# DVE's attention loop begins 21 instructions later in its stream

## The chip, the cores and the metric

The kernel runs on one core of a Trainium2 chip. The metric is the device time of one execution in microseconds, and the median of the runs is taken. The core has a matrix engine (PE, TensorE), whose weight loads are shown apart as PEld, a vector engine (DVE), a scalar engine (ACT), GpSimd (POOL) and SyncE (SP), which only issues transfers and waits. Each engine runs an instruction stream of its own, and the streams meet only at semaphores. The instructions are themselves fetched by DMA, on queues of their own (q14 and q8 in the profile).

## What is computed

A batch of 32 elements with 112 tokens of 512 numbers passes through cross-attention with 16 heads against 375 context rows, and then through a mixture of 8 experts of which each token takes two.

```python
x = x + _L0_xattn_ref(_layernorm(x), ctx_2048, mask, wq, bq, wk, bk, wv, bv, wo, bo)
x = x + _L0_ffn_ref(_layernorm(x), gate_up_proj, down_proj, router_w)

# _L0_xattn_ref: q and the output projection are quantized to 8 bits, k and v are not
q = _w8a8_linear(x, wq, bq); k = cond @ wk.T + bk; v = cond @ wv.T + bv
scores = jnp.einsum('bhnd,bhld->bhnl', q, k) * inv_sqrt_d + mask[:, None]
attn = jax.nn.softmax(scores, axis=-1)
o = jnp.einsum('bhnl,bhld->bhnd', attn, v)
return _w8a8_linear(o, wo, bo)

# _L0_ffn_ref: for each expert, weighted by the router's share of the token
gate, up = jnp.split(h @ gup.T, 2, axis=-1)
y = jax.nn.silu(gate) * up @ dp.T
```

## The kernel before

The kernel has three stages in a row: the weights are prepared (to about 34 us in the profile), attention and routing run over the batch (to about 1284 us), and then the experts run over tiles of 128 tokens.

The change is in the attention stage. All five engines follow one software pipeline there, written out by hand. In step `it` an engine works on several batch elements at once: the projections of element `it + 1`, scores, softmax and values of element `it`, the output projection of `it - 1`, and layer norm and routing of `it - 2`. Within a step each engine goes through the 16 heads in order. For one head the path is:

- PE computes `score` (L726) from `q_stack` and `k_stack`.
- DVE adds the mask and takes the minimum, an instruction that writes `probs` and a read of its accumulator that writes `neg_max` (L575). It is the first arithmetic of a step on DVE.
- ACT takes the exponential, `probs` (L499), which needs `neg_max`.
- PE turns `probs` (L734), ACT copies `probs_t` out (L492), and PE multiplies with `v` (L746).

Two banks hold scores, and PE may not compute a score before DVE has read the one two heads back (`masked`). Between the heads PE computes the projections of the next element (L761, L766).

Each engine runs the steps through the helper `iterations` (L324). Steps -3 to 2 are written out, steps 3 to 28 run in a hardware loop (`eng.Fori`), two steps a pass and 13 passes, and steps 29 to 33 are written out again. Elements 3, 5, 7 and so on to 27 start a pass. The loop's registers are set and its branch stands at L329. The waits in the loop are against a register, computed by instructions at L314. There is no barrier at the end of a pass: each engine branches back by itself. The helper `waited` (L320 to L322) is one instruction that raises a semaphore, `waits_taken`, on which nobody waits; the kernel uses it to carry a wait ahead of an instruction that has no room for it.

The streams of the built program are, in instructions of one loop body: PE 582, DVE 309, ACT 182, SP 139, POOL 96.

Of the kernel before, what the change touches and what calls it, by code (L numbers as in the profile page):

```python
# [212 lines left out]
def attention(nc, W, R, x, ctx_t, mask, x1, h2, slots):  # L213
# [19 lines left out]
    with ExitStack() as ctx:  # L233
# [72 lines left out]
        waits_taken = sem("waits_taken")  # L306
        routed, ranked, weighing, grown_made, entered = sem("routed"), sem("ranked"), sem("weighing"), sem("grown_made"), sem("entered")
        ROUTE, WEIGH = 11, 6
        counted, tabled = sem("counted"), sem("tabled")

        def need(eng, s, count):
# [8 lines left out]
        def waited(eng):  # L320

            eng.sem_inc(waits_taken, 1)  # L322

        def iterations(eng, body):  # L324

            lo, hi = 3, B - 3 - (B - 6) % 2
            for it in range(-3, min(lo, B + 2)):
                body(it, it)
            with eng.Fori(0, (hi - lo) // 2) as j:  # L329
                for k in range(2):  # L330
                    body(j * 2 + (lo + k), lo + k, True)
            for it in range(hi, B + 2):
                body(it, it)
# [215 lines left out]
        def _(dve):  # L549
            def quantize(src, amax, scale, inv, shift, ints, chain, base):  # L550

                need(dve, chain, base)
                dve.tensor_scalar(scale, amax, 1.0 / QMAX, QEPS, ALU.mult, ALU.max).then_inc(chain, 1)
                need(dve, chain, base + 1)
                dve.reciprocal(inv, scale).then_inc(chain, 1)
                need(dve, chain, base + 2)
                dve.tensor_scalar(shift, src, inv, ROUND, ALU.mult, ALU.add).then_inc(chain, 1)
                need(dve, chain, base + 3)
                dve.tensor_scalar(ints, shift, ROUND, None, ALU.subtract).then_inc(chain, 1)

            def body(it, par, inside=False):
# [4 lines left out]
                for h in range(H):  # L566
# [116 lines left out]
                    if h == 14 and has_nn:  # L683
                        need(dve, q_made, 3 * (nn - 1) + 1)
                        quantize(x_in[:, p, :], x_amax[:, :], x_scale[:, p:p + 1], x_inv[:, :], shifted[:, :], x_int[:, :], ln1, 8 * nn + 4)

            iterations(dve, body)

            def table(n, ins):
# [400 lines left out]
def program(nc, x, ctx_t, mask, wq, bq, wk_t, bk, wv_t, bv, wo, bo, gate_up_t, down_t, router_t, out):  # L1090
# [10 lines left out]
    with ExitStack() as ctx:  # L1101
# [22 lines left out]
        with ExitStack() as first:  # L1124
            sb = lambda name, shape, dt=F32: first.enter_context(nc.sbuf_tensor(name, shape, dt))
            W.update({n: sb(n, [128, 4, C], BF16) for n in ("wq_int", "wo_int")})
            W.update({n: sb(n, [128, C]) for n in ("wq_row", "wo_row", "bq_row", "bv_row", "bo_row")})
            W.update(bk_col=sb("bk_col", [128, 4]), router=sb("router", [128, 4, E]), minus_half=sb("minus_half", [128, 1]))
            W.update(stage=sb("ctx_stage", [128, 4, LP]), x_in=sb("x_in", [N, 2, C]))
            W.update(width=width, prio=sb("prio", [128, E]), regions=sb("regions", [128, E]), token=sb("token", [N, 1]),  # L1130
                     taken=sb("taken", [128, E], BF16), ones=sb("ones", [128, E]), minus_one=sb("minus_one", [128, 1]),
                     tile_no=sb("tile_no", [128, width]), tile_row=sb("tile_row", [128, width]),
                     before=sb("before", [128, 128], BF16), ones16=sb("ones16", [128, 128], BF16),
                     taken_sum=sb("taken_sum", [N, E], BF16))
            W.update({n: first.enter_context(nc.semaphore(n)) for n in ("ctx_in", "x_in_ld", "stage_pad", "c_hi_made", "c_lo_made",
                                                                        "slots_cleared", "pads_cleared")})
            prepare_weights(nc, W, x, ctx_t, wq, wk_t, wv_t, wo, bq, bk, bv, bo, router_t, slots, h2, out[T:T + PAD_ROWS, :])
            attention(nc, W, R, x, ctx_t, mask, out[0:T, :].rearrange("(b n) c -> b n c", n=N),
                      h2[0:T, :].rearrange("(b n) c -> b n c", n=N), slots)
# [29 lines left out]
```

## Time and profile before

| | |
|---|---|
| median of 3 runs | 1750.88 us (1750.59 to 1752.73) |
| the profiled execution, its time | 1751.63 us |
| its span, first to last instruction | 1749.9 us |
| PE busy | 1534.1 us, 88% |
| DVE busy | 941.4 us, 54% |
| ACT busy | 881.9 us, 50% |
| POOL busy | 732.9 us, 42% |
| granted clock of PE, mean | 0.94 of full speed |

The page gives busy shares over the whole span. They don't say which engine a stage waits for: for that the waits of an engine in a stretch are read, each with what ended it. "Issue" there stands for an idle stretch that no semaphore ended. The instructions that the sequencer handles alone (branches, registers, semaphores) are not busy time, but have their start times in the trace, and they are what shows where in its code an engine stands.

### The profile page before, as it was taken

Reading aid. Unit: us, or ns where it says so; the run is one execution under the profiler, and the core shown is the slowest. Engines: PE = TensorE matmul, PEld = TensorE weight load, DVE = VectorE, ACT = ScalarE, POOL = GpSimd, SP = SyncE. Lnnn points to the kernel's source line nnn. Section 1 sums busy time; section 2 is a strip of 40 time slices with the busy share of each in tenths; the row PEclk is TensorE's granted clock in tenths of the full one; section 3 lists DMA queues with packets and bytes.
Section 4 is the critical chain, followed back from the end, with each engine's and each line's share of the span. In section 5 each row is a group of like instructions: output and inputs, shape, how many; then the busy total and the mean of one; then the engine's idle time right before and its main releaser. Section 6 shows DMA issues by size and latency. Waiting matters only on the chain. (4 is left out here: it accounts for less than half of the span.)

```text
span 1749.9 us, 40614 instructions
## 1 busy us (share of the span) xinstructions
PE 1534.1 (88%) x11593; PEld 1336.1 (76%) x11594; DVE 941.4 (54%) x2675; ACT 881.9 (50%) x2128; POOL 732.9 (42%) x798
## 2 busy tenths in 40 slices
PE   3999988879897987989797887999549999999896
PEld 2788867768686866868686776887439999999896
DVE  6567756656575755657575665776422222222221
ACT  2566655646565655656565565666313333333232
POOL 4324434333343533334353433354335555555442
PEclk9999989889898989989898989999769999999898
DMA  6677657565565657566565756566714777756643
GB/s 202 166 205 208 171 155 211 146 187 157 151 180 147 186 146 211 138 180 168 147 173 147 212 145 186 163 178 172 246 41 85 182 170 167 177 114 141 165 74 47
DMA packets 219211, 282.02 MB, mean 161 GB/s; under 512 B 82080, under 2 KB 163872, under 8 KB 219104
## 3 DMA queue, kind: packets, MB, share of 16 engines
q1 hardware_dynamic: 200928, 247.78, 50.4%
q0 software_dynamic: 18176, 33.17, 10.7%
q14 instruction: 84, 0.69, 0.1%
q8 instruction: 23, 0.38, 0.1%
HBM read 118.12 MB, written 66.77 MB: 106 GB/s over the span
## 5 line engine op out<-in xcount | busy, mean ns | idle before, releaser
L499 ACT ACTIVATE probs<-probs,neg_max 112x375 f32<-112x375 f32 x512 | 311.7, 609 | 340.3 <-DVE neg_max L575 337.9
L575 DVE CUSTOM_DVE_ANT_0 probs<-score,neg_mask 112x375 f32<-112x375 f32 x512 | 279.2, 545 | 341.3 <-PE score L726 214.1
L734 PE MATMUL turn<-ident,probs 112*125 112x112 f32 x1536 | 274.8, 289 | 109.5 <-ACT probs L499 109.4
L734 PEld LDWEIGHTS turn<-ident,probs 112*125 112x125 f32 x1536 | 228.8, 194 | 149.9 <-ACT probs L499 118.7
L492 ACT ACTIVATE probs_t<-turn 125x336 f32<-125x336 f32 x512 | 225.2, 440 | 104.5 <-PE turn L734 102.9
L726 PE MATMUL score<-k_stack,q_stack 96*112 96x376 f32 x512 | 213.0, 416 | 5.3 <-DMA q_stack<-q_lo 4.8
L761 PE MATMUL proj<-down_hi,gate_up_hi 128*128 128x376 f32 x512 | 180.0, 351 | 7.9 <-DVE gate_up_lo L600 6.8
L761 PE MATMUL proj<-down_lo,gate_up_hi 128*128 128x376 f32 x512 | 176.7, 345 | 0.0
L761 PE MATMUL proj<-down_hi,gate_up_lo 128*128 128x376 f32 x512 | 176.1, 344 | 0.0
L975 POOL DMA_INDIRECT out<-y_rows,entries x63 | 102.2, 1622 | 175.9 <-ACT y_rows L1001 141.8
L1013 DVE TENSOR_TENSOR a_lo<-a_ps,a_hi 128x384 fp32r<-128x384 f32 x63 | 35.1, 558 | 246.2 <-ACT a_hi L988 246.2
L766 PE MATMUL proj<-gate_up_hi,down_lo 128*125 128x512 f32 x384 | 151.8, 395 | 0.0
L766 PE MATMUL proj<-gate_up_hi,down_hi 128*125 128x512 f32 x384 | 151.7, 395 | 0.0
L766 PE MATMUL proj<-gate_up_lo,down_hi 128*125 128x512 f32 x384 | 151.6, 395 | 0.0
L455 POOL TENSOR_TENSOR down_lo<-ctx_stage,down_hi 128x1504 fp32r<-128x1504 f32 x31 | 106.9, 3448 | 54.2 <-ACT down_hi L536 54.2
L761 PEld LDWEIGHTS proj<-down_hi,gate_up_hi 128*128 128x128 f32 x512 | 102.1, 199 | 14.2 <-DVE gate_up_lo L600 11.8
L746 PE MATMUL out_t<-probs_t,v 125*32 125x112 f32 x3072 | 106.3, 274 | 0.6 <-ACT probs_t L492 0.6
L460 POOL TENSOR_TENSOR w_lo<-w_raw,w_hi 128x1056 fp32r<-128x1056 f32 x32 | 79.1, 2472 | 57.3 <-ACT w_hi L544 57.3
L746 PEld LDWEIGHTS out_t<-probs_t,v 125*32 125x32 f32 x3072 | 73.8, 114 | 36.7 <-issue 22.9
L761 PEld LDWEIGHTS proj<-down_lo,gate_up_hi 128*128 128x128 f32 x512 | 101.6, 198 | 0.0
L761 PEld LDWEIGHTS proj<-down_hi,gate_up_lo 128*128 128x128 f32 x512 | 100.8, 197 | 0.0
L726 PEld LDWEIGHTS score<-k_stack,q_stack 96*112 96x112 f32 x512 | 94.5, 184 | 6.3 <-issue 6.2
(195 smaller groups left out, 3441.9 us busy)
## 6 DMA issues: line engine op xcount, KB each, us to landing
k_stack<-gate_up_hi SPq DMA_DIRECT2D x512, 94.0 KB, 2.2
k_stack<-gate_up_lo SPq DMA_DIRECT2D x256, 94.0 KB, 2.1
ctx_stage<-ctx_t SPq DMA_DIRECT2D x32, 750.0 KB
q_stack<-q_hi SPq DMA_DIRECT2D x256, 56.0 KB, 2.0
w_raw<-gate_up_t SPq DMA_DIRECT2D x32, 352.0 KB, 3.1
gate_up_dram_hi<-w_hi SPq DMA_DIRECT2D x32, 352.0 KB
gate_up_dram_lo<-w_lo SPq DMA_DIRECT2D x32, 352.0 KB
gate_up_hi<-gate_up_dram_hi SPq DMA_DIRECT2D x16, 704.0 KB, 5.4
```

The lines of the kernel that those rows point to most:

```text
L455: pool.tensor_tensor(c_lo[:, par % 2, :, :], stage[:, :, :], c_hi[:, par % 2, :, :].bitcast(F32), ALU.subtract).then_inc(c_lo_made, 1)
L460: pool.tensor_tensor(w_lo[:, :], w_raw[:, :], w_hi[:, :].bitcast(F32), ALU.subtract).then_inc(w_lo_made, 1)
L492: act.activation(probs_t[:, h % RING_T, :, :], turn[h % 2][0:LC, 0:LT * N].rearrange("p (l n) -> p l n", l=LT), ACT.Copy).then_inc(turned_ ...
L499: act.activation(probs[:, h % DS, :], probs[:, h % DS, :], ACT.Exp, bias=neg_max[:, par % 2, h:h + 1], scale=-1.0, accum_out=total[:, par ...
L575: dve.tensor_tensor_reduce(probs[:, h % DS, :], score[h % 2][0:N, 0:L], neg_mask[:, p, :], 1.0, BIG, ALU.add, ALU.min, neg_max[:, p, h:h + ...
L726: pe.matmul(score[h % 2][0:N, 0:LP], q_st[:, par % 2, h, :], k_st[:, h, :], start=True, stop=True).then_inc(scored, 1)
L734: mm = pe.transpose(turn[h % 2][0:LC, l * N:(l + 1) * N], probs[:, h % DS, l * LC:(l + 1) * LC], W["ident"][0:N, 0:N])
L746: mm = pe.matmul(out_t[QUARTER * i:QUARTER * i + QUARTER, g * N:(g + 1) * N], v[:, par % 2, l, QUARTER * h:QUARTER * h + QUARTER], probs_t ...
L761: mm = pe.matmul(bank[:, 0:LP], W[w][:, t, 128 * u:128 * u + 128], c[:, q, t, :], start=(t == 0 and w == "wk_hi" and c is c_hi), stop=(t = ...
L766: mm = pe.matmul(bank[0:LC, :], c[:, q, t, l * LC:(l + 1) * LC], W[w][:, t, :], start=(t == 0 and w == "wv_hi" and c is c_hi), stop=(t == ...
L975: pool.indirect_dma_start(out, bass.IndirectOffsetOnAxis(ap=entry[:, t - 2, 0:1], axis=0), y[:, t % 2, :], None, compute_op=ALU.add).then_ ...
L1013: dve.tensor_tensor(a_lo[:, :], a_ps[:, 0:FP], a_hi[:, :].bitcast(F32), ALU.subtract).then_inc(a_lo_made, 1)
```

## The change

Ahead of DVE's loop of the attention stage 21 calls of `waited` are put, each one semaphore increment. They stand ahead of the call of `iterations`, and so ahead of DVE's step -3 and of all that it has in this stage; the hardware loop is reached later in the same stream.

```diff
         ROUTE, WEIGH = 11, 6
+        LOOP_OFFSET = 21
         counted, tabled = sem("counted"), sem("tabled")
...
+            for _ in range(LOOP_OFFSET):
+                waited(dve)
             iterations(dve, body)
```

In the built program DVE's part of the attention stage up to the loop has 275 instructions before the change and 296 after, and the loop has 309 in both. No other engine's stream changes in length.

The listings below leave out increments and bare waits, so the 21 are not among the rows. They show DVE at the place where it enters the loop. First in the kernel before: the last rows of step 2, then the loop's set-up and its first instructions (`probs` and `neg_max` are head 0's).

```order
226 L575 ISA probs,neg_max<-score,neg_mask 112x375 [waits scored,turned]
227 L575 ISA neg_max 112x1
228 L651 TENSOR_TENSOR v<-proj,bv_row 125x512 [waits unit_made]
229 L329 UNCONDITIONAL_BRANCH
230 L329 ISA
231 L314 ISA [waits mask_negated]
232 L314 REGISTER_ALU [waits scored]
233 L575 ISA probs,neg_max<-score,neg_mask 112x375 [waits turned]
234 L575 ISA neg_max 112x1
```

The same place in the kernel after, with its line numbers one higher:

```order
226 L576 ISA probs,neg_max<-score,neg_mask 112x375 [waits scored,turned]
227 L576 ISA neg_max 112x1
228 L652 TENSOR_TENSOR v<-proj,bv_row 125x512 [waits unit_made]
229 L330 UNCONDITIONAL_BRANCH
230 L330 ISA
231 L315 ISA [waits mask_negated]
232 L315 REGISTER_ALU [waits scored]
233 L576 ISA probs,neg_max<-score,neg_mask 112x375 [waits turned]
234 L576 ISA neg_max 112x1
```

Nothing moved against anything else: the same instructions follow each other on the same waits, and only their distance from the start of DVE's stream is 21 more. An increment that is not shown stands between rows 232 and 233, so that the score instruction is the fifth of the loop.

## Rows read from the trace of the kernel before

**Rows 1.** Page: the span; an engine's busy us and share; a queue's packets, MB.

```profile
span 1749.9 us, 40614 instructions
...
PE 1534.1 (88%) x11593; PEld 1336.1 (76%) x11594; DVE 941.4 (54%) x2675; ACT 881.9 (50%) x2128; POOL 732.9 (42%) x798
...
q14 instruction: 84, 0.69, 0.1%
```

**Rows 2.** Waits of PE and DVE, 223:1100: us in total, times, longest.

```profile
PE turn L734 <- ACT probs L499: 106.8, 12, 9.5
...
DVE probs L575 <- issue: 115.0, 12, 10.1
```

**Rows 3.** Timeline of DVE, 375:391: start us, us, engine line, [idle before].

```profile
377.01 0.69 DVE L651 TENSOR_TENSOR v<-proj,bv_row 125x512 f32<-125x512 f32 x1
387.76 0.55 DVE L575 CUSTOM_DVE_ANT_0 probs<-score,neg_mask 112x375 f32<-112x375 f32 x1 [10.07 <-issue]
```

**Rows 4.** L329 and L322 on DVE, 376:388: duration ns, first and last start.

```profile
L329 DVEq COMPARE_BRANCH  x1: 68/68/68, 376.8 to 376.8; - x1
L329 DVEq FUSED_REGOPS  x1: 63/63/63, 382.7 to 382.7; - x1
...
L322 DVEq EVENT_SEMAPHORE  x1: 21/21/21, 383.0 to 383.0; - x1
```

**Rows 5.** L322 on DVE, 300:309.5, and the timeline at 309.

```profile
L322 DVEq EVENT_SEMAPHORE  x1: 21/21/21, 305.6 to 305.6; - x1
...
309.18 0.55 DVE L575 CUSTOM_DVE_ANT_0 probs<-score,neg_mask 112x375 f32<-112x375 f32 x1 [9.21 <-issue]
```

**Rows 6.** L329 on ACT, 298:310.

```profile
L329 ACTq COMPARE_BRANCH  x1: 45/45/45, 299.5 to 299.5; - x1
L329 ACTq FUSED_REGOPS  x1: 68/68/68, 299.7 to 299.7; - x1
```

**Rows 7.** Instruction queue in 376.79:382.7, 383:387.8 and 309.5:376, in this order.

```profile
q14 instruction: 1, 0.01, 0.3%
...
q14 instruction: 1, 0.01, 0.4%
...
q14 instruction: 3, 0.02, 0.1%
```

**Rows 8.** Instruction queue in 173:176 and 215.5:217; L499 on ACT, 155.4:222.9.

```profile
q14 instruction: 1, 0.01, 0.6%
...
q14 instruction: 1, 0.01, 2.0%
...
L499 ACT ACTIVATION_READ_ACCUMULATOR probs<-probs,neg_max x32: 185/187/190, 155.8 to 220.8; 112x1 f32 x32
```

**Rows 9.** Windows: length, busy PE, PEld, DVE, ACT, POOL, PE clock, DMA, GB/s.

```profile
191.00:223.00 32.00, 31.83 (x277) 26.93 (x275) 23.16 (x72) 22.33 (x56) 14.41 (x17) 1.00 0.72 196
...
309.50:318.00 8.50, 7.39 (x49) 6.63 (x50) 4.21 (x13) 5.07 (x14) 2.54 (x4) 0.57 0.43 123
```

**Rows 10.** Timeline of DVE: head 0 of elements 3, 5, 27, 29, 31.

```profile
156.53 0.55 DVE L575 CUSTOM_DVE_ANT_0 probs<-score,neg_mask 112x375 f32<-112x375 f32 x1 [0.64 <-PE score L726]
...
232.08 0.55 DVE L575 CUSTOM_DVE_ANT_0 probs<-score,neg_mask 112x375 f32<-112x375 f32 x1 [8.85 <-issue]
...
1087.14 0.55 DVE L575 CUSTOM_DVE_ANT_0 probs<-score,neg_mask 112x375 f32<-112x375 f32 x1 [9.51 <-issue]
...
1154.44 0.55 DVE L575 CUSTOM_DVE_ANT_0 probs<-score,neg_mask 112x375 f32<-112x375 f32 x1 [0.16 <-issue]
...
1221.23 0.55 DVE L575 CUSTOM_DVE_ANT_0 probs<-score,neg_mask 112x375 f32<-112x375 f32 x1 [0.16 <-issue]
```

**Rows 11.** Timeline of the start of the attention stage, 33.5:50.

```profile
35.42 0.69 DVE L655 BATCH_NORM_STATS2 stats<-x_in 112x6 f32<-112x512 f32 x1 [1.19 <-PEq L53]
...
40.76 0.44 PE L761 MATMUL proj<-down_hi,gate_up_hi 128*128 128x376 f32 x1 [0.83 <-DVE gate_up_lo L600]
```

**Rows 12.** Waits of DVE over the whole span: the handover to the experts.

```profile
DVE a L1007 <- PEq L233: 5.3, 1, 5.3
```

## The prediction

> **What bounds the kernel now.** The page comes first. PE is busy 88% of the span and DVE 54% [rows 1], so a change on DVE's stream matters only where PE waits for DVE. The table of waits over the loop of the attention stage says where that is: PE lost 106.8 us in 12 waits for ACT's `probs`, the longest 9.5 us, and DVE stood for 115.0 us in 12 waits before its score instruction (L575) that no semaphore ended, up to 10.1 us each [rows 2]. The reader is to see the 12 in both. DVE's loop runs 13 times, so it jumps back 12 times, and the stop is at each jump. The chain is short: DVE makes no `neg_max`, so ACT makes no `probs`, so PE has nothing to turn and runs dry.
>
> The timeline of DVE shows one such stop: the last work of a pass starts at 377.01, the next score instruction at 387.76, after 10.07 us of idleness put down to "issue" [rows 3]. The sequencer's own instructions divide it. The branch is at 376.8 and the first instruction of the next pass at 382.7, which is 5.9 us. The fourth instruction, the increment at L322, is at 383.0, and the fifth, the score instruction, at 387.76, another 4.8 us [rows 3, 4]. So there are two stops in a row: one on landing at the loop's first instruction and one four instructions behind it. The pass before shows the same second stop, 305.6 to 309.18, 3.6 us [rows 5]. ACT jumps back over the same iteration in 0.2 us, 299.5 to 299.7 [rows 6].
>
> What DVE waits for is its own code. A packet of the instruction queue is 0.69 MB / 84 = 8.2 KB [rows 1]. One lands in the first stop, one in the second, and three more in the rest of a pass [rows 7]. That is five per pass, and the passes repeat it.
>
> **How DVE's code lies.** In the built program DVE's loop is 309 instructions, and 309 instruction records lie between two of its branches in the trace. The second stop puts a border between two blocks of code behind the fourth instruction. The block length follows from ACT: its packets at 173:176 and 215.5:217 [rows 8] fall where its count of executed instructions is about 318 and 446, so a block holds 128. (The Trainium skill, Vector Engine (DVE) Microarchitecture Reference, section 1.2, gives 64 bytes an instruction, which makes 128 of them 8192 bytes; the trace agrees.) DVE's loop is thus cut into 4 + 128 + 128 + 49 instructions and touches four blocks. Each is fetched as the block before it is entered, so in the last one a fifth is fetched, which the loop does not need. Five packets per pass mean that none of the five survives a pass: five are more than the engine keeps.
>
> ACT tells how many it does keep. Its loop is 182 instructions in the program and 32 accumulator reads that the trace shows beside them [rows 8], 214 in all. By the same packets it starts about 63 before the border at 318, and so touches three blocks, with a fourth fetched ahead at 215.5:217 before its first branch. It then jumps back without a stop [rows 6], and the three packets of the quiet stretch 309.5:376 [rows 7] are all used up by DVE's count. So four blocks are kept, five are not.
>
> **The change.** It puts 21 semaphore increments ahead of DVE's loop and changes nothing else: the same 309 instructions run in the same order on the same waits.
>
> First term, the loop's place. Its start moves from 4 instructions before a border to 17 behind it. The last instruction is then at 17 + 309 = 326, short of the 384 at which the third block ends. The loop touches three blocks, and with the one ahead that makes four, ACT's case. Both stops go at all 12 jumps. There is room on either side: any start from 0 to 75 behind the border would do.
>
> What a jump costs today is read from the start of each pass, not from DVE's idle time, since PE also runs slower for a while after standing: it was granted 0.57 of full speed, which is close to its lower level of 1.2 GHz, over 309.5:318, and 1.00 over 191:223 [rows 9]. The first score instruction of a pass starts at 156.53 in the first and at 1087.14 in the thirteenth [rows 10]: 930.61 us for 12 passes, 77.55 each. The same pair of batch elements without a jump takes 232.08 - 8.85 - 156.53 = 66.70 us in the first pass, and 1221.23 - 1154.44 = 66.79 us in the unrolled code behind the loop [rows 10]. At 66.75 us, 12 passes take 801.0 us: a gain of 129.6 us, 10.8 per jump. The elements just behind the last jump, 1087.14 to 1154.44, took 67.30 us and should take 66.8: another 0.5 us. PE is what is late next: it is busy for 31.83 of 32 us in the undisturbed stretch 191:223 [rows 9], so nothing more than this can be had.
>
> Second term, the 21 increments. They run once, at the start of the stage, ahead of `stats` at 35.42. Three steps of DVE's sequencer took 383.0 - 382.7 = 0.3 us [rows 4], so 21 take 2.1 us. Behind them in DVE's queue stand the layer norm and quantization of element 0 and then L600, which frees PE's bank. PE already waits 0.83 us for that L600 at 40.76 [rows 11], so there is no slack and the start is later by the whole 2.1 us. What could hide some of it is a wait further on, for the first `q_stack`; I count nothing for that. No other queue is moved, and nobody waits on the semaphore that is raised. The steps written out ahead of the loop are moved too, but they run straight ahead and no block is fetched twice there.
>
> Third term, the code behind the loop. It moves by the same 21 instructions, but runs straight ahead, where each block is fetched one ahead. DVE's one jump into the experts' code stands in a barrier that lasts 5.3 us [rows 12]. It may gain or lose a stop there, at most the 5.9 us of [rows 4]. I take zero, as the other engines are in the same barrier, and keep it for the range.
>
> Sum: 1751.63 - 129.6 - 0.5 + 2.1 = 1623.6 against the profiled execution. The median of the runs, 1750.88, is 0.75 lower: 1623.
>
> **Rivals.** *One stop stays.* If fewer blocks are kept than I read from ACT, the landing at the loop's start still waits for its block; the second stop goes, since 111 instructions are left in that block to cover the next transfer. It went by 4.8 and 3.6 us in the two passes read [rows 3 to 5]; 4.2 x 12 = 50 us, so about 1703. Against it speaks ACT's jump with three blocks touched; for it, that ACT's position is worked out from packets that carry no engine's name.
> The Trainium skill speaks for this rival. Runtime: NRT & Kernel Launch, section Instruction fetch mechanics, has blocks of 16 KiB with 256 instructions, two of them held, and prefetch only straight ahead. A loop of 309 would then never be held whole, and no start would free the landing: by that rule the time is the 1703 above. The trace differs on the block (8.2 KB on DVE's queue) and on ACT's free jump over 214 instructions.
>
> *The loop does not move as said.* If what loads the code laid a loop out by its own borders, the 21 would be absorbed, both stops would stay, and the time would be 1751 to 1753. The border behind the fourth instruction speaks against it: no one would lay it so.
>
> *Slower.* The jumps stay as they are, and the increments cost their 2.1 us, with the handover to the experts catching a stop of 5.9 us that it does not have now: 1751 + 8 = 1759. It decides only where the 12 stops remain at 9 us or more; a single freed stop of 3.6 us per pass would outweigh it six times over.
>
> **How the numbers follow.** Both stops gone: 0.86. One stop stays: 0.08. No change: 0.04. Slower: 0.02. The likeliest gives 1623. Its own bounds: at the low end PE is never idle: 31.83 of 32 us [rows 9] makes a pass 0.35 us shorter, 4.2 in all; increments that are wholly hidden give 2.1, a stop that goes from the handover 5.9: 1611. At the high end a pass of 67.30 us [rows 10] is 6.6 higher, a jump that still costs the 0.2 us of ACT's on each pass 2.4, the handover 5.9 and an increment of 0.15 us each in place of 0.1 another 1.1: 1639, and 2 for the handover's own spread: 1641. Outside lie the other cases with 0.14 and a little of the first, so the range is 1611 to 1641. A measurement of this kernel can tell about 0.2% from no change. Faster by more than that is the first two cases, 0.94; within it 0.04; slower 0.02.
>
> **What would show it.** In the profile after, DVE's waits by "issue" in the loop should fall from 115.0 us in 12 to nearly none, and PE's waits for `probs` from 106.8 us to almost nothing. DVE's branch should be followed by the pass's first instruction within 0.3 us. The instruction queue should carry about 60 packets less (5 x 12), and none in a quiet stretch of the loop. Passes should start 67 us apart. PE's granted clock should be 1.00 through the loop. If one stop of about 6 us stays at each jump with three or four packets per pass, fewer than four blocks are kept and the first rival is right. If both stay, the code did not move against the borders. If the stops go but passes take 70 us or more, something other than PE is next, and the term of 66.75 is wrong.

## The result

The kernel after takes 1625.76 us in the median of 4 runs (1621.02 to 1628.82), the kernel before 1750.74 us in the median of 4 (1747.93 to 1752.73). The ratio is 0.9285, with a 95% interval of 0.9257 to 0.9313. The forecast was 1623, with a range of 1611 to 1641. The profiled execution took 1627.48 us, with a span of 1625.8.

The page of the kernel after, answering to [rows 1]: the span, busy us by engine, the granted clock of PE in 40 slices, and the instruction queue (packets, MB).

```profile
span 1625.8 us, 40635 instructions
...
PE 1506.3 (93%) x11593; PEld 1312.3 (81%) x11594; DVE 944.7 (58%) x2675; ACT 878.9 (54%) x2128; POOL 731.8 (45%) x798
...
PEclk9999999999999999999999999997599999999898
...
q14 instruction: 24, 0.20, 0.0%
```

There are 21 instructions more, the increments, and 60 code packets fewer, 84 to 24: the five of each of the 12 jumps. The waits of DVE and PE over 223:1100, answering to [rows 2] (us in total, times, longest):

```profile
DVE probs L576 <- issue: 2.1, 5, 1.0
...
PE proj L764 <- DVE gate_up_lo L601: 10.2, 26, 0.6
...
PE turn L737 <- ACT probs L500: 0.9, 3, 0.6
```

The 115.0 us of stops have come down to 2.1, and the 106.8 us that PE lost to them to 0.9. What PE waits for now is DVE's L601, which frees its bank, 0.4 us at a time. A jump of DVE, answering to [rows 3, 4] (L330 in the kernel after, window 357:362, and the timeline):

```profile
L330 DVEq COMPARE_BRANCH  x1: 56/56/56, 358.5 to 358.5; - x1
L330 DVEq FUSED_REGOPS  x1: 63/63/63, 358.8 to 358.8; - x1
...
359.62 0.55 DVE L576 CUSTOM_DVE_ANT_0 probs<-score,neg_mask 112x375 f32<-112x375 f32 x1 [0.26 <-PE score L729]
```

The first instruction of the pass follows the branch after 0.3 us instead of 5.9, and the score instruction waits only for PE's score. Head 0 of elements 3, 5, 27, 29 and 31, answering to [rows 10]:

```profile
158.82 0.55 DVE L576 CUSTOM_DVE_ANT_0 probs<-score,neg_mask 112x375 f32<-112x375 f32 x1 [0.28 <-PE score L729]
...
225.84 0.55 DVE L576 CUSTOM_DVE_ANT_0 probs<-score,neg_mask 112x375 f32<-112x375 f32 x1 [0.26 <-PE score L729]
...
960.04 0.55 DVE L576 CUSTOM_DVE_ANT_0 probs<-score,neg_mask 112x375 f32<-112x375 f32 x1 [0.26 <-PE score L729]
...
1026.81 0.55 DVE L576 CUSTOM_DVE_ANT_0 probs<-score,neg_mask 112x375 f32<-112x375 f32 x1 [0.16 <-issue]
...
1093.50 0.55 DVE L576 CUSTOM_DVE_ANT_0 probs<-score,neg_mask 112x375 f32<-112x375 f32 x1 [0.15 <-issue]
```

These five starts place the whole difference of the two profiled spans, 1749.9 - 1625.8 = 124.1 us:

| stretch | before | after | difference |
|---|---|---|---|
| to element 3 | 156.53 | 158.82 | +2.3 |
| 12 passes, element 3 to 27 | 930.61 | 801.22 | -129.4 |
| element 27 to 29 | 67.30 | 66.77 | -0.5 |
| element 29 to 31 | 66.79 | 66.69 | -0.1 |
| element 31 to the end | 528.7 | 532.3 | +3.6 |

The windows of the 12 passes, which differ by 129.0 us (930.0 to 801.0), show what the 129.4 us consist of. First the kernel before, then the kernel after (length, busy PE, PEld, DVE, ACT, POOL, granted clock, DMA share, GB/s):

```profile
157.00:1087.00 930.00, 818.99 (x6774) 694.37 (x6772) 596.11 (x1776) 549.66 (x1392) 371.79 (x434) 0.93 0.62 170
```

```profile
159.00:960.00 801.00, 791.20 (x6769) 671.19 (x6767) 598.91 (x1776) 546.52 (x1393) 369.41 (x432) 1.00 0.71 195
```

PE's idle time fell from 111.0 to 9.8 us, which is 101.2 of the 129.0. The other 27.8 us are PE's busy time, 819.0 to 791.2 for the same matmuls (6774 and 6769 records). The granted clock goes with it: its mean over the passes was 0.93, with 0.57 in the 8.5 us behind one stop [rows 9], and is 1.00 now. Whoever counts only the idle time of the stops misses a fifth of the gain.

### The profile page after: what moved, and what is told of

Same layout as the page of the kernel before. It is cut to its first block and busy times, and to the rows that moved or that the text cites. A ratio compares the mean times of both kernels' runs of the same rounds, so it can differ in the third digit from the quotient of the medians.

```text
span 1625.8 us, 40635 instructions
## 1 busy us (share of the span) xinstructions
PE 1506.3 (93%) x11593; PEld 1312.3 (81%) x11594; DVE 944.7 (58%) x2675; ACT 878.9 (54%) x2128; POOL 731.8 (45%) x798
## 3 DMA queue, kind: packets, MB, share of 16 engines
HBM read 118.12 MB, written 66.77 MB: 114 GB/s over the span
## 5 line engine op out<-in xcount | busy, mean ns | idle before, releaser
L737 PE MATMUL turn<-ident,probs 112*125 112x112 f32 x1536 | 265.7, 282 | 2.7 <-ACT probs L500 2.7
L737 PEld LDWEIGHTS turn<-ident,probs 112*125 112x125 f32 x1536 | 223.6, 189 | 37.6 <-issue 19.1
L729 PE MATMUL score<-k_stack,q_stack 96*112 96x376 f32 x512 | 208.5, 407 | 4.3 <-DMA q_stack<-q_lo 3.4
L764 PE MATMUL proj<-down_hi,gate_up_lo 128*128 128x376 f32 x512 | 172.1, 336 | 0.0
L764 PE MATMUL proj<-down_lo,gate_up_hi 128*128 128x376 f32 x512 | 172.0, 336 | 0.0
L435 POOL TENSOR_SCALAR neg_mask<-neg_mask 112x375 f32<-112x375 f32 x32 | 16.9, 528 | 268.9 <-DMA neg_mask<-mask 268.9
L764 PEld LDWEIGHTS proj<-down_hi,gate_up_hi 128*128 128x128 f32 x512 | 97.7, 191 | 24.6 <-DVE gate_up_lo L601 22.9
L749 PE MATMUL out_t<-probs_t,v 125*32 125x112 f32 x3072 | 100.8, 264 | 0.6 <-ACT probs_t L493 0.6
L1004 ACT ACTIVATE y_rows<-y_ps,row_share 128x512 f32<-128x512 f32 x63 | 43.3, 688 | 106.9 <-PE y_ps L1085 96.8
L1052 PE MATMUL gate_ps<-gate_up_hi,h_hi 128*128 x252 | 87.7, 348 | 12.1 <-SPq L950 10.2
```

What stands on the lines that cost most here:

```text
L729: pe.matmul(score[h % 2][0:N, 0:LP], q_st[:, par % 2, h, :], k_st[:, h, :], start=True, stop=True).then_inc(scored, 1)
L737: mm = pe.transpose(turn[h % 2][0:LC, l * N:(l + 1) * N], probs[:, h % DS, l * LC:(l + 1) * LC], W["ident"][0:N, 0:N])
L749: mm = pe.matmul(out_t[QUARTER * i:QUARTER * i + QUARTER, g * N:(g + 1) * N], v[:, par % 2, l, QUARTER * h:QUARTER * h + QUARTER], probs_t ...
L764: mm = pe.matmul(bank[:, 0:LP], W[w][:, t, 128 * u:128 * u + 128], c[:, q, t, :], start=(t == 0 and w == "wk_hi" and c is c_hi), stop=(t = ...
L1052: mm = pe.matmul(ps[:, 0:F], h[:, par, 128 * k:128 * k + 128], R[w][:, bass.ds(place * (KT * F2) + (k * F2 + i * F), F)], start=(k == 0 an ...
```

## The experiments

The theory after the result: code is fetched in blocks of 128 instructions, the next block is fetched when one is entered, and DVE keeps four. A loop that touches three blocks is held whole, and one that touches four is not. Against it stand three rivals: the increments help in some other way, the limit is the loop's length, or only a border close behind the loop's start costs. All kernels differ from the kernel after by the number or the place of increments alone, and compute everything. For each, the number of blocks touched follows from the start, which is 4 before a border in the kernel before.

### Both edges of the free range

The edits are one number:

```diff
-        LOOP_OFFSET = 21
+        LOOP_OFFSET = 3      # off3; 4, 79 and 80 in the others
```

> The loop begins 3 instructions later than in the kernel before, so its first instruction is the last of a block and the second one opens the next. Theory (blocks of 128, four kept, one fetched ahead): four blocks touched and a fifth fetched, both stops stay, 12 stops of 9 to 10 us, five packets per pass, about 84 on the queue, 1751 us. Rival (the increments help by what they do at the start of the stage, or any shift does): about 1625 us.

> One increment more than in off3: the loop's first instruction opens a block. Theory: three blocks touched and one ahead, no stop, passes of 66.8 us, about 24 packets; 1626 less the 17 increments saved at 0.11 us each, 1624 us. Rival (the border is not exactly where I put it): still 1751 us, as off3.

> The loop begins 75 behind a border and its branch is the last instruction of the third block. Theory: still no stop; passes of 66.8 us, about 24 packets, and 58 increments more than in the kernel after at 0.11 us, 6 us: 1632 us. Rival (fewer instructions are kept than four blocks of 128): stops are back, 1700 us or more.

> One increment more than in off79: the branch alone stands in a fourth block, and a fifth is fetched ahead when it is reached. Theory: the landing stop of about 6 us is back at each of 12 jumps, but no second stop, as 52 instructions of the first block are left to cover the next transfer; some 60 packets more than off79, passes of 73 us, about 1632 + 12 x 6.6 = 1711 us. Rival (only a border close behind the loop's first instruction costs anything): as off79, 1632 us.

Measured: off3 1754.32 us, off4 1628.90, off79 1638.88, off80 1726.57, one run each, with the kernel before at 1750.11 on the same chip. The waits of DVE before its score instruction by "issue" over the 12 passes, and the instruction queue in the same stretch, of off3 (157:1090):

```profile
DVE probs L576 <- issue: 118.4, 13, 10.6
...
q14 instruction: 65, 0.53, 0.2%
```

of off4 (157:961):

```profile
DVE probs L576 <- issue: 0.9, 1, 0.9
...
q14 instruction: 8, 0.07, 0.0%
```

of off79 (168:971):

```profile
DVE probs L576 <- issue: 3.5, 4, 0.9
...
q14 instruction: 7, 0.06, 0.0%
```

and of off80 (165:1063):

```profile
DVE probs L576 <- issue: 82.0, 13, 7.1
...
q14 instruction: 64, 0.52, 0.3%
```

One instruction decides at either edge, and it is the instruction that the block count names: 125 us between 3 and 4, 88 us between 79 and 80. Each of these is a single run, but the repeated runs of one kernel on one chip lie about 9 us apart at most (off4's five, below). This rules out the rival that any shift helps. The edges also measure the stretch that fits: a loop of 309 fits with 0 to 75 instructions between the border and its start, so from the border at its start to the one that it may not cross it is 309 + 75 = 384 instructions, three blocks of 128. In off80 only the branch lies in the fourth block and the first border comes 52 instructions behind the start, where DVE doesn't stop, and yet each jump costs: so a border close behind the start isn't the only thing that does. The jump of off80 at 380 shows the single stop (L330, window 379.5:391, and the timeline):

```profile
L330 DVEq COMPARE_BRANCH  x1: 68/68/68, 380.3 to 380.3; - x1
L330 DVEq FUSED_REGOPS  x1: 63/63/63, 387.4 to 387.4; - x1
...
387.86 0.55 DVE L576 CUSTOM_DVE_ANT_0 probs<-score,neg_mask 112x375 f32<-112x375 f32 x1 [7.02 <-issue]
```

Two sizes were missed. Off80 was expected at 1711 us and took 1726.57: its passes take (1062.17 - 165.59) / 12 = 74.7 us, 7.9 more than a free one, where 6.6 was expected. Off79 was expected at 1632 and took 1638.88: its first score comes at 70.26 against 62.26 in the kernel after, 8.0 us for 58 increments where 6 was expected. Off128, below, has its first score at 73.13, 10.9 us for 107 increments or 0.10 each, so that about 2 us of off79's start belong to that one execution. They are less than a third of its miss of 6.9 us. Between the first score and element 3 it loses another 1.5 us against the kernel after, over the passes 0.6 and behind element 31 1.5, and the forecast of 1632 started from 1626 where the profiled execution of the kernel after took 1627.48.

### Position alone, and increments alone

Off128 has 128 increments at the same place (`LOOP_OFFSET = 128`), so that the loop lies against the borders as in the kernel before. Behind21 has the 21 behind DVE's loop:

```diff
-            for _ in range(LOOP_OFFSET):
-                waited(dve)
             iterations(dve, body)
+            for _ in range(LOOP_OFFSET):
+                waited(dve)
```

> 128 increments ahead of DVE's part of the stage: the loop lies against the borders exactly as in the kernel before, one block later. Theory (only the place against the borders matters): both stops are back, 12 of 9 to 10 us, some 85 packets, passes of 77.5 us; with 107 increments more than in the kernel after, at 0.14 us each by off79, the first score is 15 us later than there, so about 1751 + 17 = 1768 us. Rival (any large enough distance from the stream's start frees the loop): 1626 + 15 = 1641 us.

> The same 21 increments behind DVE's part of the stage, ahead of its table of tiles: the loop stays where it is in the kernel before. Theory: both stops stay, passes of 77.5 us, about 84 packets; 1751 us and up to 3 us for the increments, which delay the table. Rival (it is the increments, not the loop's place): about 1625 us.

Measured: off128 1764.15 us, behind21 1756.64, the kernel before 1746.48 on the same chip. The passes of off128 (170:1097), then those of behind21 (156:1086), are as slow as before:

```profile
DVE probs L576 <- issue: 111.6, 12, 10.2
...
q14 instruction: 65, 0.53, 0.2%
```

```profile
DVE probs L576 <- issue: 114.7, 12, 10.5
```

Increments that leave the loop where it was give nothing, and a whole block more of them brings every stop back. What counts is the place of the loop against borders that repeat every 128 instructions. Off128 was expected at 1768, with a first score 15 us later than in the kernel after; it came 10.9 us later. Behind21 is 3 us above the expected ceiling of 1754, and 10 above the kernel before on its own chip. It isn't the loop, whose passes take 77.4 us. From element 31 to the end it takes 535.5 us against 528.7 in the kernel before, and PE's waits for the experts' weights (L950) are 11.8 us of that against 6.0. This wait differs from trace to trace (below).

### Length of the loop

In grow29 and grow30 the start is that of the kernel after and the loop is longer, by 29 or 30 increments in each of its two steps:

```diff
                 for h in range(H):
+                    if inside and h > 0:
+                        for _ in range(2 if h < H - 1 else 29 - 28):   # 30 - 28 in grow30
+                            waited(dve)
```

> The kernel after with its loop 58 instructions longer (29 increments in each of the two steps of a pass, two behind each of heads 1 to 14's beginning and one at head 15), 367 in all: begun 17 behind a border it ends with the third block's last instruction. Theory: no stop and about 24 packets, as in off79, with whatever the increments cost DVE's sequencer, 0.1 us each where PE waits for DVE and nothing elsewhere: 1626 to 1660 us. Rival (it is the loop's length that is limited, not the number of blocks that it touches, and 309 was close to the limit): stops as in off80, 90 us more.

> 60 instructions more in the loop instead of 58, 369 in all: its last two stand in a fourth block. Theory: one landing stop per jump is back, as in off80, 12 x 7.9 = 95 us more than grow29, and some 60 packets more. Rival (as under grow29: length alone): no difference between the two beyond 0.2 us per pass.

Measured: grow29 1639.66 us and grow30 1725.05, 85 us apart, where 95 were expected. The instruction queue in the 12 passes of grow29 (159:970), and then DVE's wait and the queue in those of grow30 (159:1062):

```profile
q14 instruction: 7, 0.06, 0.0%
```

```profile
DVE probs L579 <- issue: 102.8, 73, 7.4
...
q14 instruction: 64, 0.52, 0.2%
```

A loop of 367 instructions runs without a stop, one of 369 does not, and one of 309 does not either if it begins badly. So it isn't the length that is limited, but the blocks that it touches. Grow29's passes take (969.82 - 159.95) / 12 = 67.5 us, so its 58 instructions cost 0.7 us a pass, where 58 increments of 0.093 us (below) would take 5.4 if nothing hid them. DVE has the room, as it waits 120.0 us of these 12 passes for PE's scores. Grow30's passes take (1061.75 - 159.62) / 12 = 75.2 us, 7.7 more than grow29's and close to the 7.9 expected. What is missing of the 95 us lies behind element 31, where grow30 takes 526.2 us and grow29 534.2 (see the third term).

### The price of one landing, and the smallest offset

Off104 (`LOOP_OFFSET = 104`) begins 100 behind a border. The other two runs time the smallest free offset against the kernel after.

> The loop begins 100 behind a border and ends 25 instructions into the fourth block. In off80 the branch followed at once on the entry of the fourth block, so that the packet fetched ahead and the one waited for were under way together, and the landing took 6.5 to 7.1 us instead of 5.9. Theory (the two packets stand in each other's way): here the packet ahead is in before the branch, the landing takes 5.9 us as in the kernel before; the 28 instructions left in the first block cover most of the next transfer; passes of 73.5 to 74 us. Rival (a landing is simply dearer when DVE has fewer instructions of slack, or varies by run): 6.5 to 7.1 us again, passes of 74.7 us or more.

> off4 again, timed: 17 increments fewer than in the kernel after, whose first score came 1.5 us later than off4's. Theory: 1.5 us less than the kernel after, 0.1%, which these rounds may not be able to tell; 0.93 of the kernel before.

> The kernel after on the same chip, for the comparison with off4: theory 1626 us, 1.5 us above off4.

Measured: off104 1707.70 us, with the kernel before at 1758.51 on this chip. Its passes take (1043.70 - 168.24) / 12 = 73.0 us. One jump of it (L330, window 375:384, and the timeline):

```profile
L330 DVEq COMPARE_BRANCH  x1: 68/68/68, 376.0 to 376.0; - x1
L330 DVEq FUSED_REGOPS  x1: 63/63/63, 381.7 to 381.7; - x1
...
382.14 0.55 DVE L576 CUSTOM_DVE_ANT_0 probs<-score,neg_mask 112x375 f32<-112x375 f32 x1 [5.25 <-issue]
```

The landing takes 5.7 us here and 7.1 in off80. Over the 11 jumps behind the first it is 5.5 to 6.3 us in off104, 6.0 in the mean, and 6.5 to 7.2 in off80, 6.9 in the mean. The instruction queue between the branch and the landing shows what differs, in off80 (380.3:387.4) and in off104 (376.0:381.7):

```profile
q14 instruction: 2, 0.02, 0.9%
...
q14 instruction: 1, 0.01, 0.3%
```

In off80 the packet fetched ahead in the last block and the one that the jump waits for come together, and in off104 the packet ahead starts 2.8 us before the branch and is in by then. So a jump is dearer where the two meet; whether they share a transfer's way or are served one after the other, the traces don't tell. This is 0.9 of the 1.3 us per jump by which off80 was dearer than expected, and the rest isn't traced. Off104's passes are also 0.5 us below the 73.5 to 74 expected: DVE's waits by "issue" there are 61.0 us in 11, all at the jump, so the 28 instructions left in the first block covered all of the next transfer.

Off4 took 1623.74 us (5 runs, 1623.29 to 1632.36) and the kernel after 1625.32 (5 runs, 1623.35 to 1627.61). Their ratios to the kernel before are 0.9257 (0.9235 to 0.9279) and 0.9244 (0.923 to 0.9257). The medians are 1.6 us apart, but the runs of the two overlap, so the 1.5 us that off4 should save can't be told from these runs. The gain itself is confirmed on this chip.

## Why the prediction was right

**What bounds the kernel.** Right as read: the 12 stops of DVE before its score were what PE waited for, and both vanished together.

**The cause.** Right. The step that carried it was to split an "issue" wait by the sequencer's instructions and to set it beside the packets of the instruction queue. The counts of blocks, drawn from five packets per pass on DVE and ACT's free jump over 214 instructions, held to the instruction at both edges (0 and 75 behind the border).

**First term.** 129.6 us were forecast and 129.4 measured, a pass of 66.75 us against 66.77. It came out so closely because the price was taken from starts of passes, with the two undisturbed pairs as the measure, and so held the lower clock after a stop without naming its size. The 0.5 us at elements 27 to 29 was 0.5. The price was sound, but that it hit to 0.2 us is in part luck. The passes of the kernels with all stops take between 77.2 us (off128) and 77.7 (off3), a spread of 7 us over 12 passes, and on the chip of the timed runs the medians differ by 133.2 us where they differed by 125.0 in the result.

**Second term.** 2.1 us were forecast and 2.3 measured. The increments start from 34.9 to 36.8, in steps of 0.093 us (the kernel after, L323, window 33:37):

```profile
L323 DVEq EVENT_SEMAPHORE  x21: 21/21/21, 34.9 to 36.8; - x21
```

The whole delay reached the first score, which starts at 62.26 where it was 59.93. That fits the reading that there was no slack before L600.

**Third term.** Taken as zero, and 3.6 us were lost behind element 31. It isn't the handover: DVE's wait there is 4.7 us against 5.3 in [rows 12]. It is PE's wait for the weights of an expert, in the kernel before and in the kernel after:

```profile
PE gate_ps L1049 <- SPq L947: 6.0, 1, 6.0
```

```profile
PE gate_ps L1052 <- SPq L950: 10.2, 1, 10.2
```

The lines explain most of the 3.6 us, but not whether they come from the change. Over all the traces this wait is 8.7 to 10.2 us in four of the six whose loop runs free (after, off4, off79, grow29) and 5.5 and 5.8 in the two timed ones. With stops it is 4.7 to 6.0 in five of seven, and 9.3 and 11.8 in off128 and behind21. From element 31 to the end the six free ones take 528.8 to 534.2 us, and the seven with stops 526.2 to 532.3 and, in behind21, 535.5. The two groups overlap, but their medians are 533.0 and 528.7. So a small part of the gain may be lost again there, a term that the prediction has at nothing; no run here isolates it, and why the weights come sooner in one execution than in another is open.

**Rivals.** *One stop stays* was wrong for this offset, and is what happens from 80 on. Its price was given as 1703 us, 6.6 us a jump. Off104 is this case and pays 6.2 a jump, with 1707.70 us in all; off80 pays 7.9. The page of the Trainium skill that spoke for it, Runtime: NRT & Kernel Launch, section Instruction fetch mechanics, is at odds with these runs for DVE: by its two blocks of 256 instructions, the one being run and the one ahead, off4 and off79 could not be free of stops, and neither could grow29 with a loop of 367. That a branch whose target is not held has to wait for it is what it says and what off80 shows. *The loop does not move* and *slower* did not occur. Under *slower* a freed stop of 3.6 us per pass was said to outweigh the 8 us six times over; 43.2 against 8 is five times, which changes no chance.

**What would show it.** Each sign came: nearly no stop (2.1 us), 60 packets fewer and none in the quiet stretch 309.5:376, 0.3 us to the first instruction, 67 us a pass, a granted clock of 1.00.

## What to carry to other kernels

Where a loop's engine shows one idle stretch per pass that no semaphore ended, look for the sequencer's branch, the first instruction behind it and the packets of the instruction queue: if the packets come in every pass, the loop is not held. It helps to move its start, by a few idle instructions ahead of it, until it touches one block fewer, and any edit ahead of a loop can undo that without a trace in the diff; so look at the packets per pass after each. Price such a stop by the distance between passes and not by the idle time, since here a fifth of the gain was PE's busy time, longer at the lower granted clock behind the stops.

## What the runs showed of the hardware

- In this kernel DVE holds four blocks of 128 instructions, one of them fetched ahead: a loop is free if it touches three. The edge is sharp: 3 and 4 instructions of offset give 1754.32 and 1628.90 us, 79 and 80 give 1638.88 and 1726.57.
- A jump to a block that is not held takes 5.4 to 6.5 us in this stage behind the first jump (before, off3, off104, off128, behind21), and 6.4 to 7.3 where the packet ahead is under way with it (off80 and grow30). The first jump is shorter in the five, 2.9 (off128) to 5.1 us (behind21), but not in the two, 6.5 and 7.5. What makes that difference wasn't tried.
- A stop of DVE cost more than its length: 12 stops of 115.0 us in all made the passes 129.4 us longer.
